# Up-projection weights of expert tile pairs: from copies of a resident set on ScalarE to two transfers a pair into three buffers

## What is computed

```
x      = x + attn_block(layernorm(x))            # RWKV: time mix (a scan over tokens), then channel mix
xm     = layernorm(x)
scores = xm @ gate_w.T                           # [tokens, 8]
top 2 of the 8, softmax over the two -> probability per token and expert
h12    = xm @ w12[e].T                           # w12: [8, 512, 128]; h1, h2 = first and last 256
hidden = silu(h1) * h2
y      = sum over the two experts of prob * (hidden @ w3[e].T)   # w3: [8, 128, 256]
out    = x + y
```

## Time and profile before

| | |
|---|---|
| median of 3 timed runs | 349.14 us (349.12 to 349.5) |
| span of the profiled execution, its own time | 381.7 us |
| TensorE busy | 279.6 us (73%) |
| VectorE busy | 249.1 us (65%) |
| GpSimd busy | 215.2 us (56%) |
| ScalarE busy | 196.8 us (52%) |
| moved by DMA | 29.08 MB, mean 76 GB/s |
| `w_up` copies on ScalarE (line 618) | 72, 41.6 us |

### The profile page before, as it was taken

How to read it: one execution, slowest core, us unless ns; L and a number is a source line. 1 busy time by engine, 2 the same in 40 slices (tenths; PEclk the granted TensorE clock), 3 DMA queues, 4 the chain that set the end, 5 groups by cost and what they waited for, 6 DMA issues and landing times.

```text
span 381.7 us, 6770 instructions
## 1 busy us (share of the span) xinstructions
PE 279.6 (73%) x1697; PEld 217.7 (57%) x1698; DVE 249.1 (65%) x790; ACT 196.8 (52%) x413; POOL 215.2 (56%) x227
## 2 busy tenths in 40 slices
PE   0685899989979699695943317987887898887720
PEld 0233475748575566464622106987887887887610
DVE  3089998998899959883544701646654654645675
ACT  3445688776867556644610022646664664645300
POOL 5142465277886768858747730454565565465482
PEclk9996699998989679968795586999999999999955
DMA  8900000001011001111111213232222222232774
GB/s 287 396 12 2 0 2 27 2 36 43 34 42 42 28 33 45 35 44 42 54 35 58 86 49 79 55 82 65 68 80 70 68 78 71 62 85 61 249 255 186
DMA packets 22406, 29.08 MB, mean 76 GB/s; under 512 B 4317, under 2 KB 15583, under 8 KB 22128
## 3 DMA queue, kind: packets, MB, share of 16 engines
q1 hardware_dynamic: 14832, 13.45, 12.1%
q0 software_dynamic: 4352, 8.47, 6.7%
q10 hardware_dynamic: 3200, 6.90, 4.8%
HBM read 15.09 MB, written 12.14 MB: 71 GB/s over the span
## 4 chain that ended last, share of the span: by engine, by line
issue 25%; DVE 23%; POOL 8%; another core or an unknown queue 8%; PE 7%; ACT 5%; DMA 4%; ACTq 4%; SPq 3%; DVEq 1%; POOLq 0%
POOL rows_d L416 4%; ACTq L615 3%; DVE rden L886 3%; DVE st L825 3%; ACT w_up L618 3%; PE p_up L799 2%; DMA o_all<-res_d 2%; DVE num L880 2%; DVE den L876 2%; DVE spots L974 1%; PE p_f L726 1%; DVE mv L832 1%; DMA res_d<-yo,result_row 1%; ACT xgT L609 1%
## 5 line engine op out<-in xcount | busy, mean ns | idle before, releaser
L441 POOL DMA_INDIRECT res_d<-yo,result_row x72 | 71.2, 990 | 71.7 <-DVE yo L1071 53.0
L416 POOL DMA_INDIRECT rows_d<-rows,pos x64 | 67.3, 1052 | 22.6 <-issue 22.6
L799 PE MATMUL p_up<-xgT,w_up 128*128 128x128 f32 x576 | 71.8, 279 | 0.0
L799 PEld LDWEIGHTS p_up<-xgT,w_up 128*128 128x128 f32 x576 | 68.8, 196 | 0.0
L1056 DVE SCALAR_TENSOR_TENSOR gate_h<-th,p_up 128x512 f32<-128x512 f32 x36 | 24.8, 688 | 46.3 <-issue 24.1
L618 ACT ACTIVATE w_up<-w_exp 128x512 f32 x72 | 41.6, 623 | 14.3 <-issue 13.4
L714 PE MATMUL p_up<-ysum,w_sb 128*128 128x512 f32 x64 | 36.4, 678 | 5.0 <-POOL ysum L395 5.0
L603 ACT ACTIVATE th<-p_up 128x512 f32<-128x512 f32 x36 | 21.4, 595 | 30.9 <-remote 13.8
L726 PEld LDWEIGHTS p_f<-wfv_half,kk 128*128 128x128 f32 x256 | 34.3, 210 | 5.2 <-issue 4.9
L726 PE MATMUL p_f<-wfv_half,kk 128*128 128x128 f32 x256 | 35.1, 294 | 0.0
L789 PE MATMUL p_tr<-ident,xg 128*128 128x128 f32 x72 | 14.9, 289 | 21.0 <-ACT xgT L609 10.9
(11 more groups left out here) (153 smaller groups left out, 568.2 us busy)
## 6 DMA issues: line engine op xcount, KB each, us to landing
xg<-rows_d SPq DMA_DIRECT2D x72, 65.0 KB
o_all<-res_d SPq DMA_DIRECT2D x16, 256.0 KB, 6.8
w_exp<-experts ACTq DMA_DIRECT2D x1, 3072.0 KB, 17.1
x_all<-x SPq DMA_DIRECT2D x10, 256.0 KB, 2.3
out<-x_all ACTq DMA_DIRECT2D x8, 256.0 KB, 2.4
x_all<-x SPq DMA_DIRECT2D x1, 1536.0 KB, 16.4
res_d<-yo,result_row POOLq DMA_INDIRECT x72
rows_d<-rows,pos POOLq DMA_INDIRECT x64
```

The lines of the kernel that those rows point to most:

```text
L416: pool.indirect_dma_start(out=rows_d[:, :], out_offset=bass.IndirectOffsetOnAxis(ap=row, axis=0), in_=rows_of[is_last(c)][:, t, k, :], in_ ...
L441: pool.indirect_dma_start(out=res_d[:, :], out_offset=bass.IndirectOffsetOnAxis(ap=row, axis=0), in_=yo[u][:, n, :], in_offset=None, bound ...
L799: mm = pe.matmul(p_up[u % 2][:, n, h * P:(h + 1) * P], w_up[u % 2][:, n, h * P:(h + 1) * P], xgT[u % 2][:, n, :], start=True, stop=True)
```

## The change

The experts' weights are split into two inputs. `down` (8 x 256 columns, 1024 KB) is loaded at the start into `w_down`, in place of the 3072 KB of `w_exp`; `up` (8 x 512 columns) stays in DRAM. For each pair ScalarE no longer copies two blocks of 128 x 512 inside SBUF but issues two transfers of 128 x 512 float32 (256 KB each, rows of 2 KB, 16 KB apart in DRAM) on its queue, into one of three buffers `w_up`, each with a semaphore of its own. `up` on TensorE waits for that semaphore. ScalarE's wait for the resident set ahead of the loop goes; the slot table's columns count in units of the down-projection, so the up-projection's column is twice that.

```
-EW = 2 * H + 2 * D
+UPW = 2 * H
+DNW = 2 * D
+WBUFS = 3
-        w_exp = sb("w_exp", [P, E * EW])
+        w_down = sb("w_down", [P, E * DNW])
-        w_up = [sb(f"w_up{n}", [P, 2, 2 * H]) for n in range(2)]
+        w_up = [sb(f"w_up{n}", [P, 2, UPW]) for n in range(WBUFS)]
 # ScalarE, start
-            act.dma_start(w_exp[:, :], experts_in).then_inc(S["experts_in"], 16)
+            act.dma_start(w_down[:, :], down_in).then_inc(S["experts_in"], 16)
 # ScalarE, ahead of the loop
-            act.wait_ge(S["experts_in"], 16)
 # ScalarE, expert_weights(q, _, u)
                 act.load(loaded, slot_w[0:1, bass.ds(q * 2, 2)])
+                first_col = [act.snap(value, min_val=0, max_val=(E - 1) * DNW) for value in loaded]
+                after(act, "up_done", q - WBUFS + 1)
                 for n in range(2):
-                    first_col = act.snap(loaded[n], min_val=0, max_val=(E - 1) * EW)
-                    act.activation(w_up[u % 2][:, n, :], w_exp[:, bass.ds(first_col, 2 * H)], ACT.Copy)
+                    act.dma_start(w_up[u % WBUFS][:, n, :], up_in[:, bass.ds(first_col[n] * (UPW // DNW), UPW)])\
+                        .then_inc(S[f"w_up_in{u % WBUFS}"], 16)
 # TensorE, up(q, r, u)
                 after(pe, "xgT_ready", q + 1)
+                after(pe, f"w_up_in{u % WBUFS}", r * (32 * BUFS // WBUFS) + 32 * (u // WBUFS + 1))
-                        mm = pe.matmul(p_up[u % 2][:, n, h * P:(h + 1) * P], w_up[u % 2][:, n, h * P:(h + 1) * P],
+                        mm = pe.matmul(p_up[u % 2][:, n, h * P:(h + 1) * P], w_up[u % WBUFS][:, n, h * P:(h + 1) * P],
 # TensorE, down(q, _, u)
-                                       w_exp[:, bass.ds(first_col[n] + (2 * H + j * D), D)],
+                                       w_down[:, bass.ds(first_col[n] + j * D, D)],
```

More of the change, by code:

```diff
@@ L41, with build @@
 BUFS = 6
+WBUFS = 3
 EARLY = 3
 NOWHERE = 2 * RESULTS
-def build(nc, x_in, w_in, v_in, experts_in, out):
+def build(nc, x_in, w_in, v_in, up_in, down_in, out):
     ctx = ExitStack()
@@ L154, in build @@
         names += [f"{n}{b}" for n in ("xg_loaded", "scattered") for b in range(BUFS)]
+        names += [f"w_up_in{b}" for b in range(WBUFS)]
         S = {n: sem(n) for n in names}
@@ L790, in turn_rows, with up @@
                 mm.then_inc(S["xg_T"], 1)
-            def up(q, _, u):
+            def up(q, r, u):
                 after(pe, "xgT_ready", q + 1)
+                after(pe, f"w_up_in{u % WBUFS}", r * (32 * BUFS // WBUFS) + 32 * (u // WBUFS + 1))
                 for n in range(2):
                     for h in range(2 * H // P):
-                        mm = pe.matmul(p_up[u % 2][:, n, h * P:(h + 1) * P], w_up[u % 2][:, n, h * P:(h + 1) * P],
+                        mm = pe.matmul(p_up[u % 2][:, n, h * P:(h + 1) * P], w_up[u % WBUFS][:, n, h * P:(h + 1) * P],
                                        xgT[u % 2][:, n, :], start=True, stop=True)
@@ L805, in down @@
                 pe.load(loaded, slot_w[0:1, bass.ds(q * 2, 2)])
-                first_col = [pe.snap(value, min_val=0, max_val=(E - 1) * EW) for value in loaded]
+                first_col = [pe.snap(value, min_val=0, max_val=(E - 1) * DNW) for value in loaded]
                 after(pe, "hid_ready", q + 1)
@@ L1033, in _ @@
             link(dve.tensor_reduce(slot_e[:, :], past[:, :, :], mybir.AxisListType.X, ALU.add))
-            dve.tensor_scalar(slot_w[:, :], slot_e[:, :], float(E - 1), float(EW), ALU.min, ALU.mult)\
+            dve.tensor_scalar(slot_w[:, :], slot_e[:, :], float(E - 1), float(DNW), ALU.min, ALU.mult)\
                 .then_inc(S["table_w"], 1)
@@ L1100 @@
         "vecs": np.stack([a[n] for n in VEC], axis=1),
-        "experts": np.concatenate([a["w12"].transpose(2, 0, 1),
-                                   a["w3"].transpose(2, 0, 1).reshape(2, P, E, D).transpose(1, 2, 0, 3).reshape(P, E, 2 * D)],
-                                  axis=2).reshape(P, E * EW),
+        "up": a["w12"].transpose(2, 0, 1).reshape(P, E * UPW),
+        "down": a["w3"].transpose(2, 0, 1).reshape(2, P, E, D).transpose(1, 2, 0, 3).reshape(P, E * DNW),
     }
```

## The result

The changed kernel takes 375.26 us, median of 4 runs (373.49 to 378.64), against 349.31 us (349.12 to 349.5) for the kernel before in the same session: a ratio of 1.0767, 95% interval [1.0713, 1.0822]. It is slower, by 26 us; 357.4 us were predicted, and the range ended at 369. The direction and the new wait were forecast; its cost was put at 8.3 us, a third of what it is.

What follows compares the result with a forecast made beforehand. TensorE at 2.90 us a pass was taken to bound the expert loop, VectorE the start. 349.14 - 4.5 (start) + 12.8 (new wait) = 357.4 us; range 344 to 369, the forecast's own range 350 to 366.

Steps and rivals of the forecast that it cites:

- the new wait: Expert loop: TensorE's up block waits for its pair's transfers; 0.38 us a pass over 34 passes, 12.8 us lost.
- The bound of the kernel before: Expert loop: TensorE's own 2.90 us a pass in timed runs; the profile's holes belong to that one execution.
- the copies: Expert loop: ScalarE's 72 weight copies, 1.25 us a pass, lie beside TensorE's work; removing them gains nothing.
- The start: Kernel start: a smaller resident set lets x land earlier, VectorE's first product at 20.2; 4.5 us gained.
- Landing: Expert loop: time from a pair's first transfer issue until its second has landed; 3.5 us taken.
- The step from tanh to the first issue: Expert loop, ScalarE: from tanh through slot register load, column multiplication and buffer wait to the first DMA issue; 0.95 us.
- The prediction's bound for a landing with the row loads and scatters beside it: Expert loop: a pair's landing if row loads and scatters take a third of the DMA engines; 3.8 us.
- the row from DRAM: Kernel start, profile row: 256 KB from DRAM with a neighbour landed in 3.5 us, matching the landing taken.
- its data part: Expert loop, landing: moving a pair's 524 KB at 346 GB/s takes 1.5 us, besides 1.5 us fixed.
- the estimate: Expert loop: the Trainium skill's fit gives a pair's landing 3.2 us, and 7.7 us of loss instead of 12.8.
- I cost these at nothing: Ahead of the expert loop: four transfers loading the first two pairs replace four copies; cost 0.
- the ring: Expert loop: up(q), tanh, register load, issues, landing, up(q+2); 6.55 us for two passes, against 5.80 available.

Runs made afterwards that it cites:

- e8: The kernel before, unchanged, profiled once more: 348.57 us, span 346.5.
- e6: The kernel before without the weight copies inside the loop (68 of 72; most results wrong): 348.88 us, ratio 1.0044.
- e4: The kernel before, with its 3072 KB resident set issued on SP's queue behind the bulk of x, loop untouched: 345.99 us, ratio 0.9891.
- e12: Repeat of e4, the kernel before with its resident set issued behind the bulk of x: 343.81 us, ratio 0.9858.
- e10: e1's kernel, with pairs 1 and 2 loaded ahead of the loop only after the first pair's row loads have landed: 350.0 us, ratio 1.0044.
- e1: The changed kernel with transfers issued three pairs ahead instead of two, three pairs loaded ahead of the loop: 350.66 us, ratio 1.0052.
- e5: The changed kernel with each pair's transfers issued before ScalarE's tanh instead of behind it, still two pairs ahead: 355.96 us, ratio 1.0244.
- e2: The changed kernel with each transfer cut to 256 of 512 columns (128 KB), other halves zero: 355.53 us, ratio 1.0189.
- e7: e4's kernel plus four unused transfers of 256 KB issued by ScalarE ahead of the loop, copies kept: 348.49 us, ratio 1.0028.
- e11: e1's kernel with only pair 0 loaded ahead of the loop, the second and third pairs issued behind turned rows: 347.38 us, ratio 0.9959.
- e3: The changed kernel with SP's first eight result loads held back until the last pair's weights have landed: 373.58 us, ratio 1.0728.
- e9: The changed kernel with the second pair's transfers issued ahead of the loop only after the first pair's row loads landed: 375.82 us, ratio 1.0785.

## Why the prediction was off

*The bound of the kernel before* was read rightly: 2.90 us a pass (e8), the copies free (e6). A small misreading: in rows 4 one interval of 2.94 us is followed by one of 4.38, not two of 2.9 by a hole.

*The start* was right in size. 4.5 us were taken; alone it is worth 3.8 to 5.0 in the timed runs (e4, e12), and slot_row gains 4.0 in the change's profile. What the working left out is the dense weights: it gave the value projection its old end, 20.09. In the kernels with the change's start the first product stands at 20.4 to 21.7 where `w_sb` landed 7.2 to 7.4 us after its issue, and at 23.1 and 23.7 where it took 10.2 and 9.9 us (e10, e1).

*The new wait* was right as a mechanism: the chain shows its links in the predicted order, and an earlier issue removes it (e1, e5). *Landing* is the mis-sized term: 3.5 us taken, 3.99 measured from the first issue. With 3.99 the prediction's own sum gives 365.7 us, still within its range; what carried the time beyond 369 are terms that it put at nothing or did not have, below. The step from tanh to the first issue gave back 0.14 (0.95 taken, 0.81 measured), the release took 0.14 again. 0.56 us a pass over 29 ordinary passes is 16.3 us; at 0.38 they would have been 11.0. The prediction's bound for a landing with the row loads and scatters beside it, 3.8 us, was nearer than the row from DRAM that it chose. The 346 GB/s of its data part was worked out from 318 at a share of 0.92; the result loads themselves ran at 318. The Trainium skill's page "DMA: Bandwidth & Descriptors", section "Anatomy of one DMA", by whose fit the estimate was 3.2 us, is further off; it is a fit for GpSimd's path and for one DMA, where here two of ScalarE's are in flight beside row loads and scatters. The Trainium skill's same page, "Rules for kernel authors", issue early and wait late, is borne out by e1 (2.90 us a pass).

*"I cost these at nothing"*, of the four transfers ahead of the loop, is the step that failed in kind. The prediction saw that the loop's start hangs on SP's row loads and did not ask what the transfers do to these: from the first row load's issue to the first transposes pass 2.8 us with the copies (215.95 to 218.77, e8) and 7.1 with the transfers (212.11 to 219.25). The loop's start was 4.1 us longer; half the bytes bring 3.4 of it back (e2), the transfers alone cost 2.4 there (e7), and issuing the later ones behind the first turned rows gains 2.6 net (e11 against e1).

*Not in the sum* at all were the loop's end (6.6 us in the trace), where the last weights meet the result loads: the path there was taken for an ordinary pass, though rows 10 had 6.2 us and more for 256 KB in the queue of eight result loads. Nor were the passes around 254.58 (3.9 us). Both are waits of about 2 us or more, and the half clock after them adds 1.4 to 1.7 us each to the block that follows. What made the one in the middle late is open: its pair landed 5.6 us after its first issue (248.91), and no run isolated it; e3 and e9 do not have it. By e3 the end's 6.6 us are not all to be had back: part of them turns up after the loop.

Sum: predicted were 12.8 - 4.5 = 8.3 us, the profiles differ by 27.4. Of the 19.1 us between them the landing has 5.3 (16.3 - 11.0), the other passes 10.1 (1.4 + 3.9 + 6.6, less the 1.8 that the forecast gave them), the transfers ahead of the loop 4.1 and the start 0.5; the tail gives back 0.9. The forecast's own range allowed for the landing alone. The 5.3 and the 3.9 are one split of the ring's loss: e3 and e9 lose nearly as much in it (18.8 and 19.4 us over 31 passes, here 20.2) without the passes around 254.58.

## What to carry to other kernels

A third buffer hides nothing unless the issue moves with it: follow the issuing engine's program order back from the transfer to the instruction ahead of it, close the ring through the consumer, and compare it with that many passes. Count each new transfer where it meets others too: bulk loads ahead of a loop delay the small loads that start it, and the last ones of a loop meet whatever is loaded next. If the gain of a change comes from the start alone, try the start alone: here reordering one transfer gave it without the loop.

## What the runs showed of the hardware

Small row loads suffered beside bulk transfers: from their issue to the transposes that use them 2.8 us pass in the unchanged kernel (215.95 to 218.77), and 7.8 with six transfers of 256 KB issued ahead of them (214.71 to 222.55, e1). The DMA engines stood at a share of 0.88 without TensorE waiting, with the issue three pairs ahead (e1). One profiled execution was unlike the timed runs: 381.7 us and 3.55 us a pass, then 346.5 and 2.90 the next time, of the same kernel; why is open.
